# Patch embedding of a small vision model: f32 products replaced by three products of rounded high and low parts

## The chip, the cores and the metric

The kernel runs on one core of one Trainium2 chip. The metric is the device time of one execution in microseconds. Three executions of the kernel before took 379.61, 381.12 and 382.11 us, so the median is 381.12 us. One execution was also recorded by the hardware profiler; it took 379.39 us.

## The reference

The program is a vision tower: patch embedding, layer norm, two small causal attentions, a mixture of 32 experts (8 chosen per token) with a shared one, a full attention, and a quantised feed-forward block, with residuals. Only the first step matters here:

```
x = data.reshape(b, C, HP, P, WP, P)                      # 16 images, 3 x 96 x 96, P = 16
x = x.transpose(0, 2, 4, 1, 3, 5).reshape(b, N, F)        # N = 36 patches of F = 768 numbers
x = jnp.einsum('bnf,df->bnd', x, W_lin) + b_lin           # W_lin is 256 x 768
cls = jnp.broadcast_to(class_token, (b, 1, D))
out = jnp.concatenate([cls, x], axis=1) + position_embeddings
```

So 576 patches, with a column left free for each of the 16 class tokens, make T = 592 token columns. The product has an inner length of 768 and 256 results per token. All of it is float32.

## The kernel before, in words

Features lie on the 128 partitions and tokens along the free axis. The 592 tokens are worked in two halves of 296 columns (`half(hf)`), and the 256 model features in two chunks of 128 (`c`). The inner length of 768 is cut into KT = 6 pieces of 128. One SBUF tensor, `region`, holds the six pieces of patches (`patches`, 128 x 592 each) and the six pieces of weights (`w_lin_sb`, 128 x 256 each). Later stages use the same memory for other things.

Each engine has its own program, and semaphores join them. At the start:

- SyncE issues the six patch transfers (L340), then weights of the two attentions and of the last feed-forward block (L341 to L346), and waits for the embedding before it issues more (L347, L348).
- ScalarE issues three weight pieces (L532), then the constants `cst`, `vec` and `nt` (L533 to L535), then the other three weight pieces (L537), then three small attention weights (L538 to L540). Only after these twelve issues does it reach its first computation. That is a one-element activation whose purpose is to load the activation table of the next function (`load_table`, L550); it stands behind waits for the constants.
- VectorE clears `zeros` (L874), waits for the constants, converts some of them to bf16 (`cstb`, L876, which also completes `s_init`), adds two tables into `posb` (L877), waits for the embedding's sums half by half (`s_tok`) and adds `posb` to them (`h`, L882).
- TensorE runs 16 products on zeros ahead of the data (`keep_busy`, START_BUSY = 16). Then it takes the pieces k = 0 to 5 in order. For each it waits until patches and weights have landed (`s_x[k]`) and issues four f32 products, half 0 then half 1, chunk 0 then chunk 1, into four accumulators in PSUM. The last piece tells VectorE when half 0 and half 1 are summed.
- GpSimd sets a few small buffers (L399 to L405) and waits for the embedding.

After that follows the first norm: TensorE sums the means of `h` half by half (`s_h`), VectorE subtracts (`xc`, L777), ScalarE squares (`sq`, L562), TensorE sums the squares, ScalarE and VectorE make the scale, and VectorE applies it (`xn`, L792). Every step waits for the one before, for half 0 first. Every matmul of the kernel is recorded at one helper line, L1090.

In the expert stage of the kernel, products are already made of parts: ScalarE copies a tile into float32r, a rounded 32-bit format (`wh`, `ah`, `xh`: the high part), another engine subtracts the rounded copy from the original (`wl`, `al`, `xl`: the low part), and TensorE adds high x high, high x low and low x high (`three`). `split_all` is the float32r buffer of that stage and is not used before it.

Of the kernel before, what the change touches and what calls it, by code (L numbers as in the profile page):

```python
# [9 lines left out]
T = B * S  # L10
D = 256
P = 128
C = D // P
KT = 3 * PATCH * PATCH // P
HEADS, KVH, HD = 16, 4, 16
LAT = 64
HALF = T // 2
# [24 lines left out]
LEAD = 3  # L42
ATTENTION_BUSY = 5

QK_UNITS = ((0, 0), (1, 0), (2, 0), (2, 1), (0, 1), (1, 1))
ACT_VARIANTS = 2
WPIECES, VPIECES = 8, 8
WPIECE, VPIECE = C * FF // WPIECES, B * D // VPIECES
VZ = 1 + VPIECES
# [28 lines left out]
def program(nc, x, w_lin, consts, consts_bf, vecs, g_wq, g_down, g_k, g_v, g_wo, l_wq, l_wk, l_wv, l_wo,  # L78
            gate_w, experts, qkv_w, out_w, w1, w2, weights, out):
    f32, f32r, bf16 = mybir.dt.float32, mybir.dt.float32r, mybir.dt.bfloat16  # L80
    ALU, ACT, AX = mybir.AluOpType, mybir.ActivationFunctionType, mybir.AxisListType

    with ExitStack() as ctx:
        def sb(name, shape, dt=f32):
            return ctx.enter_context(nc.sbuf_tensor(name, shape, dt))

        def sem(name):
            return ctx.enter_context(nc.semaphore(name))
# [4 lines left out]
        patches = region[:, 0:KT * T].rearrange("p (k t) -> p k t", k=KT)  # L93
        w_lin_sb = region[:, KT * T:KT * (T + D)].rearrange("p (k d) -> p k d", k=KT)
# [79 lines left out]
        split_all = sb("split_all", [P, 2 * NRING * EW], f32r)  # L174
# [3 lines left out]

        pairs_r = split_all[:, 0:P]

        wb_flat = wb[:].rearrange("p r t -> p (r t)")
        qvar = [[z.rearrange("p (g t) -> p g t", g=4) for z in zs] for zs in
                ([wb_flat[:, c * C * T:(c + 1) * C * T] for c in range(C)],
# [22 lines left out]
        ps = [psum[:, i, :] for i in range(8)]  # L206

        def const(name, rows=P):
            a, b = CONST_COLS[name]
            return cst[0:rows, a:b]  # L210
# [8 lines left out]
        def half(hf):  # L219
            return slice(hf * HALF, (hf + 1) * HALF)  # L220
# [3 lines left out]


        s_x = [sem(f"patches_loaded{k}") for k in range(KT)]
        s_cst = sem("constants_loaded")
        s_attn_w = [sem(f"attention_weights_loaded{a}") for a in range(2)]
        s_wo_w = sem("output_weights_loaded")
# [292 lines left out]
        def _(act_e):  # L522
# [5 lines left out]
                ins.then_inc(s_act_own, 1)  # L528
                act_e.wait_ge(s_act_own, own[0])

            for k in range(LEAD):
                act_e.dma_start(w_lin_sb[:, k, :], w_lin[:, k, :]).then_inc(s_x[k], 16)  # L532
            act_e.dma_start(cst[:], consts).then_inc(s_cst, 16)  # L533
            act_e.dma_start(vec[:], vecs).then_inc(s_cst, 16)
            act_e.dma_start(nt[:, 0:NBF], consts_bf).then_inc(s_cst, 16)  # L535
            for k in range(LEAD, KT):
                act_e.dma_start(w_lin_sb[:, k, :], w_lin[:, k, :]).then_inc(s_x[k], 16)  # L537
            act_e.dma_start(down_sb[:], g_down).then_inc(s_attn_w[0], 16)  # L538
            act_e.dma_start(gk_sb[:], g_k).then_inc(s_attn_w[0], 16)
            act_e.dma_start(gv_sb[:], g_v).then_inc(s_attn_w[0], 16)  # L540
            act_e.wait_ge(s_init, 8)
            act_e.wait_ge(s_cst, 48)

# [34 lines left out]
            def key_variants(a, hf):  # L578

                act_e.wait_ge(s_qk, a * NPROJ + QK_UNITS.index((2, hf)) + 1)  # L580
                if a == 1:
                    act_e.wait_ge(s_s, PAIRS)
                for g in range(ACT_VARIANTS):
                    ins = nc.scalar.activation(km[:, 0, g, half(hf)], sq[:, 0, half(hf)], ACT.Copy,  # L584
# [128 lines left out]
            for hf in range(2):  # L713
                for m in range(C):
                    ins = nc.scalar.activation(h[:, m, half(hf)], ps[2 * m + hf][:, 0:HALF], ACT.Copy)
# [13 lines left out]
            for b in range(4):  # L729
# [3 lines left out]
                for j in range(2):  # L733
                    rows = slice(64 * j, 64 * j + S)
                    ins = nc.scalar.activation(v16[rows, 4 * b:4 * b + 4, :, j, :],
                                               ps[VALUE_BANKS[b]][rows, :].rearrange("p (i h d) -> p i h d", i=4, h=HEADS // 2),
                                               ACT.Copy)
# [24 lines left out]
        def _(dve):  # L762
# [8 lines left out]
            def bc(ap, dims):  # L771
                return ap.broadcast_to(dims)
# [39 lines left out]
            def qk_units(a):  # L812
# [6 lines left out]
                for u in range(NPROJ + 1):  # L819
# [22 lines left out]
                    if u >= 2 and QK_UNITS[u - 2][0] == 2:  # L842

                        hf = QK_UNITS[u - 2][1]
                        for g in range(ACT_VARIANTS, 4):
                            ins = nc.vector.tensor_scalar(km[:, 0, g, half(hf)], sq[:, 0, half(hf)],
# [25 lines left out]


            nc.vector.memset(zeros[:], 0.0).then_inc(s_zero, 1)  # L874
            dve.wait_ge(s_cst, 48)
            nc.vector.tensor_copy(cstb[:], nt[:, 0:NBF]).then_inc(s_init, 1)  # L876
            link(nc.vector.tensor_tensor(posb[:].rearrange("p c s -> p (c s)"), vector("pos"), vector("base"),  # L877
                                         ALU.add))
            for hf in range(2):
                dve.wait_ge(s_tok, hf + 1)  # L880
                for c in range(C):
                    ins = nc.vector.tensor_tensor(  # L882
                        h[:, c, half(hf)].rearrange("p (b s) -> p b s", s=S),
                        ps[2 * c + hf][:, 0:HALF].rearrange("p (b s) -> p b s", s=S),
                        bc(posb[:, c, :].unsqueeze(1), [P, HB, S]), ALU.add)
# [6 lines left out]
            for a in range(2):  # L892
# [8 lines left out]
                for hf in range(2):  # L901
# [3 lines left out]
                    for m in range(C):  # L905
                        ins = nc.vector.tensor_tensor((x0, tmp)[a][:, m, half(hf)], x0[:, m, half(hf)],
                                                      ps[4 + 2 * m + hf][:, 0:HALF], ALU.add)
# [29 lines left out]
            for t in range(TT):  # L937
                for g in range(GROUPS):
                    ins = nc.vector.max(top[:, t, g, :], choice[:, t, g * PER_GROUP:(g + 1) * PER_GROUP])
# [19 lines left out]
            for t in range(TT):  # L959
                ins = nc.vector.max(top[:, t, 0, :], masked[:, t, :])  # L960
            link(ins)
            for t in range(TT):
                ins = nc.vector.match_replace(repl[:, t, :], top[:, t, 0, :], masked[:, t, :], -3.0e38)
# [44 lines left out]
            for hf in range(2):  # L1008
# [5 lines left out]
                for c in range(C):  # L1014
                    for g in range(4):
                        ins = nc.vector.tensor_scalar(kvar[:, c, g, half(hf)], kt[:, c, half(hf)],
                                                      const("onehot4")[:, g:g + 1], None, ALU.mult)
# [16 lines left out]
            for hf in range(2):  # L1034
                dve.wait_ge(s_wo, 4 + hf + 1)
                for m in range(C):
                    ins = nc.vector.scalar_tensor_tensor(h[:, m, half(hf)], ps[4 + 2 * m + hf][:, 0:HALF],
                                                         outb[:, m:m + 1], h[:, m, half(hf)],
                                                         ALU.add, ALU.add)
# [16 lines left out]
            for ch in range(FC):  # L1056
                dve.wait_ge(s_hid, ch + 1)
                ins = nc.vector.tensor_reduce(peak[:, ch:ch + 1], hid[:, ch, :], AX.X, ALU.max,
                                              apply_absolute_value=True)
# [6 lines left out]
            for ch in DVE_CHUNKS:  # L1066
                ins = nc.vector.tensor_scalar(hid[:, ch, :], hid[:, ch, :], inv[:, 3:4], ROUND, ALU.mult, ALU.add)
# [8 lines left out]
            for m in range(C):  # L1076
                ins = nc.vector.tensor_scalar(x0[:, m, :], h[:, m, :], b2s[:, m:m + 1], None, ALU.add)
            link(ins)
            for hf in range(2):
                dve.wait_ge(s_f2, hf + 1)  # L1080
                for m in range(C):
                    ins = nc.vector.scalar_tensor_tensor(x0[:, m, half(hf)], ps[2 * m + hf][:, 0:HALF], sxw[:, 1:2],
                                                         x0[:, m, half(hf)], ALU.mult, ALU.add)
# [4 lines left out]
        def _(pe):  # L1088
            def mm(out_, lhsT, rhs, start, stop):
                return nc.tensor.matmul(out_, lhsT, rhs, start=start, stop=stop, skip_group_check=True)  # L1090
# [273 lines left out]
            pe.wait_ge(s_zero, 1)  # L1364
            keep_busy(7, START_BUSY, zeros[:, 0:P], zeros[:, 0:HALF])
            for k in range(KT):
                pe.wait_ge(s_x[k], 32)
                for hf in range(2):
                    for c in range(C):
                        ins = mm(ps[2 * c + hf][:, 0:HALF], w_lin_sb[:, k, c * P:(c + 1) * P],  # L1370
                                 patches[:, k, half(hf)], k == 0, k == KT - 1)
                    if k == KT - 1:
                        ins.then_inc(s_tok, 1)


            pe.wait_ge(s_init, 8)
# [29 lines left out]
            for t in range(TT):  # L1406
                if t == HALF // P:
                    pe.wait_ge(s_xn, 6)
                for c in range(C):
                    ins = mm(ps[6][:, t * EXPERTS:(t + 1) * EXPERTS], xn[:, c, t * P:(t + 1) * P],  # L1410
                             gate_sb[:, c, :], c == 0, c == C - 1)
# [75 lines left out]
            for u in range((UNITS - 1) // NRING * NRING, UNITS):  # L1487
                i = u % NRING
# [10 lines left out]
            for hf in range(2):  # L1499
                pe.wait_ge(s_xn, 6 + hf + 1)  # L1500
                for part in range(2):
                    for c in range(C):
                        bank = ps[4 * (1 - part) + 2 * c + hf][:, 0:HALF]
                        for k in range(C):
                            ins = mm(bank, qkv_sb[:, k, part * D + c * P:part * D + (c + 1) * P],
                                     xn[:, k, half(hf)], k == 0, k == C - 1)
# [12 lines left out]
            for ch in range(FC):  # L1519
                if ch >= 2:  # L1520
                    pe.wait_ge(s_hid, ch - 1)
                for hf in range(2):
                    for c in range(C):
                        ins = mm(ps[4 + 2 * (ch % 2) + hf][:, 0:HALF], w1q[:, c, ch * P:(ch + 1) * P],
                                 xq[:, c, half(hf)], c == 0, c == C - 1)
# [6 lines left out]
            for n, ch in enumerate(order):  # L1532
# [4 lines left out]
                for hf in range(2):  # L1537
                    for m in range(C):
                        ins = mm(ps[2 * m + hf][:, 0:HALF], w2q[:, ch, m * P:(m + 1) * P],
                                 hidq[:, ch, half(hf)], n == 0, n == FC - 1)  # L1540
# [128 lines left out]
```

## Time and profile before

| what | value |
|---|---|
| median of three executions | 381.12 us |
| profiled execution, its own time | 379.39 us |
| span of the profiled execution, first to last instruction | 377.6 us |
| mean granted TensorE clock | 0.995 |
| TensorE matmul busy | 349.9 us, 93% |
| TensorE weight load busy | 292.7 us, 78% |
| VectorE busy | 231.7 us, 61% |
| ScalarE busy | 179.4 us, 48% |
| GpSimd busy | 137.5 us, 36% |

The span is 1.8 us shorter than the time of the same execution; the rest lies before its first and after its last instruction. Matmul records overlap, since a matmul lasts longer than the distance to the next one, so the distance between starts is the rate. An f32 product of the program appears as two MATMUL records, a float32r or bf16 product as one. Busy shares are averages over stages with different limits; the change concerns the first 18 us of 377.6.

### The profile page before, as it was taken

Reading aid. Unit: us, or ns where it says so; the run is one execution under the profiler, and the core shown is the slowest. Engines: PE = TensorE matmul, PEld = TensorE weight load, DVE = VectorE, ACT = ScalarE, POOL = GpSimd, SP = SyncE. Lnnn points to the kernel's source line nnn. Section 1 sums busy time; section 2 is a strip of 40 time slices with the busy share of each in tenths; the row PEclk is TensorE's granted clock in tenths of the full one; section 3 lists DMA queues with packets and bytes.
Section 4 is the critical chain, followed back from the end, with each engine's and each line's share of the span. In section 5 each row is a group of like instructions: output and inputs, shape, how many; then the busy total and the mean of one; then the engine's idle time right before and its main releaser. Section 6 shows DMA issues by size and latency. Waiting matters only on the chain.

```text
span 377.6 us, 9798 instructions
## 1 busy us (share of the span) xinstructions
PE 349.9 (93%) x3916; PEld 292.7 (78%) x3916; DVE 231.7 (61%) x495; ACT 179.4 (48%) x353; POOL 137.5 (36%) x144
## 2 busy tenths in 40 slices
PE   8999898899898899999999999999999999889664
PEld 6655665568667899999999999999997788656333
DVE  0265689786879355555555555555554663666686
ACT  0156944487473244444444444444445774224270
POOL 0035852270260266665656544443310013410021
PEclk9999999999999999999999999999999999999899
DMA  8940001000550224444454544545200000000001
GB/s 295 366 144 0 3 6 30 0 3 3 169 169 2 90 97 142 141 146 148 148 147 148 143 139 127 146 133 152 80 1 2 0 2 3 5 3 0 0 2 66
DMA packets 14865, 32.08 MB, mean 85 GB/s; under 512 B 2480, under 2 KB 4464, under 8 KB 14576
## 3 DMA queue, kind: packets, MB, share of 16 engines
q1 hardware_dynamic: 12592, 29.66, 24.8%
q10 hardware_dynamic: 2240, 1.95, 1.5%
q8 instruction: 24, 0.39, 0.4%
q14 instruction: 9, 0.07, 0.1%
HBM read 30.91 MB, written 0.69 MB: 84 GB/s over the span
## 4 chain that ended last, share of the span: by engine, by line
PE 72%; DVE 14%; ACT 5%; DMA 3%; issue 3%; ACTq 1%; DVEq 0%
PE psum L1090 72%; DMA region<-in_w_lin 2%; DVE xn L792 1%; DVE rc L857 1%; DVE nt L786 1%; ACT region L749 1%; DVE nt L788 1%; DVE nt L789 1%; DMA wb<-weights 1%; DVE km L1072 1%; ACT km L584 1%; DVE pk L797 1%; DVE xc L777 1%; ACT sq L562 1%; ACT ars L565 1%
## 5 line engine op out<-in xcount | busy, mean ns | idle before, releaser
L1090 PE MATMUL psum<-xh,split_all 128*128 128x296 f32 x544 | 122.6, 299 | 1.8 <-DVE rt L986 1.8
L464 POOL TENSOR_TENSOR split_all<-km,split_all 128x768 fp32r<-128x768 f32 x34 | 63.7, 1876 | 85.0 <-ACT split_all L670 85.0
L1090 PEld LDWEIGHTS psum<-xh,split_all 128*128 128x128 f32 x544 | 91.7, 188 | 2.3 <-DVE rt L986 2.1
L1090 PE MATMUL psum<-xl,split_all 128*128 128x296 f32 (+1 forms) x288 | 85.1, 300 | 0.2 <-ACT e L641 0.2
L690 ACT ACTIVATE ah<-rt 128x296 fp32r<-128x296 f32 x68 | 30.7, 451 | 78.4 <-DVE rt L986 71.9
L1090 PEld LDWEIGHTS psum<-xl,split_all 128*128 128x128 f32 (+1 forms) x288 | 53.1, 187 | 1.1 <-POOL xl L507 0.4
L988 DVE TENSOR_TENSOR al<-rt,ah 128x296 fp32r<-128x296 f32 x64 | 30.0, 468 | 33.1 <-ACT ah L690 33.1
L1090 PE MATMUL psum<-ah,split_all 128*128 128x296 f32 x272 | 48.4, 300 | 1.3 <-ACT ah L690 1.3
L983 DVE TENSOR_TENSOR rb<-psum,wb 128x296 f32<-128x296 f32 x64 | 29.9, 467 | 31.8 <-ACT psum L688 28.1
L1090 PEld LDWEIGHTS psum<-ah,split_all 128*128 128x128 f32 x272 | 40.6, 188 | 1.8 <-ACT ah L690 1.8
L986 DVE TENSOR_TENSOR rt<-rb,psum 128x296 f32<-128x296 f32 x64 | 29.6, 463 | 5.2
L688 ACT ACTIVATE psum<-psum 128x296 f32<-128x296 f32 x64 | 25.7, 401 | 12.9 <-PE psum L1090 12.7
L670 ACT ACTIVATE split_all<-km 128x768 fp32r<-128x768 f32 x34 | 28.3, 833 | 4.2 <-DMA km<-in_experts 4.1
L1090 PE MATMUL psum<-al,split_all 128*128 128x296 f32 x136 | 29.9, 301 | 0.1
L641 ACT ACTIVATE e<-psum 101x592 f32<-101x592 f32 x24 | 15.7, 663 | 24.4 <-PE psum L1090 24.3
L507 POOL TENSOR_TENSOR xl<-mx,cst 128x592 fp32r<-128x592 f32 x8 | 9.6, 1199 | 46.0 <-DVE mx L1027 46.0
L1090 PE MATMUL psum<-cstb 128*128 128x296 bf16 (+1 forms) x196 | 25.8, 303 | 0.0
L1090 PEld LDWEIGHTS psum<-al,split_all 128*128 128x128 f32 x136 | 22.2, 189 | 0.6 <-POOL al L470 0.6
L1090 PE MATMUL psum<-region 128*128 128x296 f32 x80 | 21.5, 420 | 0.8 <-DMA region<-in_w_lin 0.4
L857 DVE RECIPROCAL rc<-psum 128x148 f32<-128x148 f32 x16 | 17.3, 1082 | 8.0 <-PE psum L1090 6.4
L1090 PEld LDWEIGHTS psum<-cstb 128*128 128x128 bf16 (+1 forms) x196 | 14.9, 101 | 8.9 <-issue 4.0
L1090 PE MATMUL psum<-sq,cst 128*128 128x296 f32 x64 | 19.6, 425 | 1.0 <-ACT sq L562 0.8
(176 smaller groups left out, 530.7 us busy)
## 6 DMA issues: line engine op xcount, KB each, us to landing
km<-in_experts SPq DMA_DIRECT2D x34, 384.0 KB, 4.0
wb<-weights SPq DMA_DIRECT2D x32, 296.0 KB, 3.7
w_sb<-in_w SPq DMA_DIRECT2D x2, 1024.0 KB, 11.6
region<-in_x SPq DMA_DIRECT2D x6, 296.0 KB, 5.3
region<-in_w_lin ACTq DMA_DIRECT2D x6, 128.0 KB, 6.3
qkv_sb<-in_qkv_w SPq DMA_DIRECT2D x1, 768.0 KB, 4.7
cst<-in_consts ACTq DMA_DIRECT2D x1, 502.5 KB, 6.4
out<-x SPq DMA_DIRECT2D x2, 148.0 KB, 2.1
```

The costliest lines, as they stand in the source:

```text
L464: nc.gpsimd.tensor_tensor(wl[i], ring[i], wh[i].bitcast(f32), ALU.subtract)\
L507: nc.gpsimd.tensor_tensor(dg[:, p % 2, :, :], mx[:, p % 2, :].unsqueeze(2).broadcast_to([P, HEADS, S]), const("minus_ident").unsqueeze(1). ...
L562: nc.scalar.activation(sq[:, :, half(hf)], src[:, :, half(hf)], ACT.Square).then_inc(s_sq, 1)
L641: nc.scalar.activation(e[0:ROWS, p % 2, 0:EC].rearrange("p (k n) -> p k n", k=2), psum[0:ROWS, sb0:sb0 + 2, 0:HALFPOS * S], ACT.Exp, scale ...
L670: nc.scalar.activation(wh[i], ring[i], ACT.Copy).then_inc(s_wsh, 1)
L688: nc.scalar.activation(gate, ps[bank][:, 0:HALF], ACT.Silu).then_inc(s_sg, 1)
L690: nc.scalar.activation(ah[:, j, :], act[:, j, :], ACT.Copy).then_inc(s_ah, 1)
L857: link(nc.vector.reciprocal(rc[:], bank[:, G4 * S:2 * G4 * S]))
L983: nc.vector.tensor_tensor(gu[:, j, :], gate, weight, ALU.mult).then_inc(s_mulc, 1)
L986: nc.vector.tensor_tensor(act[:, j, :], gu[:, j, :], ps[5][:, 0:HALF], ALU.mult).then_inc(s_act, 1)
L988: nc.vector.tensor_tensor(al[:, j, :], act[:, j, :], ah[:, j, :].bitcast(f32), ALU.subtract)\
L1090: return nc.tensor.matmul(out_, lhsT, rhs, start=start, stop=stop, skip_group_check=True)
```

## The change

The six pieces are now converted before they are multiplied. ScalarE rounds the weight piece (128 x 256) and each half of the patch piece (128 x 296) to float32r; VectorE subtracts to get the low parts, in the same order. TensorE makes three products for each one it made before: high x high, low weight x high patches, high weight x low patches. The parts live in three slots in `split_all`; ScalarE may fill a slot again once TensorE has told it (`s_pmm`) that the products of that slot are done. The six weight transfers are issued together, ahead of the constants.

```diff
+PATCH_SLOTS = 3
...
+        PW = 2 * (T + D)
+        pslot = [split_all[:, i * PW:(i + 1) * PW] for i in range(PATCH_SLOTS)]
+        px_hi, px_lo = [s_[:, 0:T] for s_ in pslot], [s_[:, T:2 * T] for s_ in pslot]
+        pw_hi, pw_lo = [s_[:, 2 * T:2 * T + D] for s_ in pslot], [s_[:, 2 * T + D:PW] for s_ in pslot]
...
-            for k in range(LEAD):
+            for k in range(KT):
                 act_e.dma_start(w_lin_sb[:, k, :], w_lin[:, k, :]).then_inc(s_x[k], 16)
             act_e.dma_start(cst[:], consts).then_inc(s_cst, 16)
             act_e.dma_start(vec[:], vecs).then_inc(s_cst, 16)
             act_e.dma_start(nt[:, 0:NBF], consts_bf).then_inc(s_cst, 16)
-            for k in range(LEAD, KT):
-                act_e.dma_start(w_lin_sb[:, k, :], w_lin[:, k, :]).then_inc(s_x[k], 16)
             act_e.dma_start(down_sb[:], g_down).then_inc(s_attn_w[0], 16)
             act_e.dma_start(gk_sb[:], g_k).then_inc(s_attn_w[0], 16)
             act_e.dma_start(gv_sb[:], g_v).then_inc(s_attn_w[0], 16)
+            for k in range(KT):
+
+                i = k % PATCH_SLOTS
+                act_e.wait_ge(s_x[k], 32)
+                if k >= PATCH_SLOTS:
+                    act_e.wait_ge(s_pmm, k - PATCH_SLOTS + 1)
+                nc.scalar.activation(pw_hi[i], w_lin_sb[:, k, :], ACT.Copy).then_inc(s_pwh, 1)
+                for hf in range(2):
+                    nc.scalar.activation(px_hi[i][:, half(hf)], patches[:, k, half(hf)], ACT.Copy).then_inc(s_pxh, 1)
             act_e.wait_ge(s_init, 8)
             act_e.wait_ge(s_cst, 48)
...
             nc.vector.memset(zeros[:], 0.0).then_inc(s_zero, 1)
+            for k in range(KT):
+
+                i = k % PATCH_SLOTS
+                dve.wait_ge(s_pwh, k + 1)
+                nc.vector.tensor_tensor(pw_lo[i], w_lin_sb[:, k, :], pw_hi[i].bitcast(f32), ALU.subtract).then_inc(s_pwl, 1)
+                for hf in range(2):
+                    dve.wait_ge(s_pxh, 2 * k + hf + 1)
+                    nc.vector.tensor_tensor(px_lo[i][:, half(hf)], patches[:, k, half(hf)],
+                                            px_hi[i][:, half(hf)].bitcast(f32), ALU.subtract).then_inc(s_pxl, 1)
             dve.wait_ge(s_cst, 48)
...
             for k in range(KT):
-                pe.wait_ge(s_x[k], 32)
+                i = k % PATCH_SLOTS
+                pe.wait_ge(s_pwh, k + 1)
+                for hf in range(2):
+                    pe.wait_ge(s_pxh, 2 * k + hf + 1)
+                    for c in range(C):
+                        mm(ps[2 * c + hf][:, 0:HALF], pw_hi[i][:, c * P:(c + 1) * P], px_hi[i][:, half(hf)], k == 0, False)
+                pe.wait_ge(s_pwl, k + 1)
                 for hf in range(2):
                     for c in range(C):
-                        ins = mm(ps[2 * c + hf][:, 0:HALF], w_lin_sb[:, k, c * P:(c + 1) * P],
-                                 patches[:, k, half(hf)], k == 0, k == KT - 1)
+                        mm(ps[2 * c + hf][:, 0:HALF], pw_lo[i][:, c * P:(c + 1) * P], px_hi[i][:, half(hf)], False, False)
+                    pe.wait_ge(s_pxl, 2 * k + hf + 1)
+                    for c in range(C):
+                        ins = mm(ps[2 * c + hf][:, 0:HALF], pw_hi[i][:, c * P:(c + 1) * P], px_lo[i][:, half(hf)],
+                                 False, k == KT - 1)
                     if k == KT - 1:
                         ins.then_inc(s_tok, 1)
+                if k < KT - PATCH_SLOTS:
+                    ins.then_inc(s_pmm, 1)
```

## Rows read from the trace of the kernel before

**Rows 1.** Page, chain of waits by engine; then its pieces in time (start, length).
```profile
PE 72%; DVE 14%; ACT 5%; DMA 3%; issue 3%; ACTq 1%; DVEq 0%
...
3.71 7.90 DMA region<-in_w_lin
...
11.65 6.25 PE psum L1090 x24
```

**Rows 2.** Timeline, embedding and what follows: start us, length us, engine, line, operation.
```profile
5.01 6.24 PE L1090 MATMUL psum<-region 128*128 128x296 f32 x24
...
11.65 6.25 PE L1090 MATMUL psum<-region 128*128 128x296 f32 x24 [0.41 <-DMA region<-in_w_lin]
...
17.02 1.76 DVE L882 TENSOR_TENSOR h<-psum,posb 128x296 f32<-128x296 f32 x4 [5.92 <-PE psum L1090]
...
18.00 2.23 PE L1090 MATMUL psum<-h,cst 128*128 128x296 f32 x8
```

**Rows 3.** Timeline of ScalarE's queue, transfer issues, first and last among twelve.
```profile
0.74 1.38 ACTq L532 DMA_DIRECT2D region<-in_w_lin  x3
...
2.15 0.45 ACTq L533 DMA_DIRECT2D cst<-in_consts  x1
...
3.71 1.56 ACTq L537 DMA_DIRECT2D region<-in_w_lin  x3
...
6.47 0.61 ACTq L540 DMA_DIRECT2D gv_sb<-in_g_v  x1
```

**Rows 4.** Timeline of ScalarE, its first table load; then all loads grouped.
```profile
10.76 1.28 ACT L550 ACT_TABLE_LOAD   x1 [10.76 <-DMA nt<-in_consts_bf]
...
12.05 0.20 ACT L550 ACTIVATE spare<-eps 128x1 f32<-128x1 f32 x1
...
L550 ACT ACT_TABLE_LOAD x11 | 14.1, 1283 | 10.9 <-DMA nt<-in_consts_bf 10.8
```

**Rows 5.** Groups by line and shape, ScalarE (busy us, mean ns); then two timeline rows.
```profile
L690 ACT ACTIVATE ah<-rt 128x296 fp32r<-128x296 f32 x68 | 30.7, 451 | 78.4 <-DVE rt L986 71.9 <-DVE rt L932 6.5
L670 ACT ACTIVATE split_all<-km 128x768 fp32r<-128x768 f32 x34 | 28.3, 833 | 4.2 <-DMA km<-in_experts 4.1
...
40.88 0.45 ACT L611 ACTIVATE rs<-rs 128x296 f32<-128x296 f32 x1
41.23 0.96 ACT L584 ACTIVATE km<-sq,cst 128x296 f32<-128x296 f32 x2
```

**Rows 6.** Groups by line and shape, VectorE, the subtractions of the expert stage.
```profile
L988 DVE TENSOR_TENSOR al<-rt,ah 128x296 fp32r<-128x296 f32 x64 | 30.0, 468 | 33.1 <-ACT ah L690 33.1
L923 DVE TENSOR_TENSOR xl<-xn,xh 128x592 fp32r<-128x592 f32 x2 | 1.5, 770 | 0.1
```

**Rows 7.** Busy by stretch: length; PE, PEld, DVE, ACT, POOL; PEclk, DMA, GB/s.
```profile
5.02:17.90 12.88, 12.47 (x49) 8.93 (x48) 1.23 (x4) 1.49 (x2) 0.00 (x0) 1.00 1.05 406
180.00:200.00 20.00, 20.00 (x149) 20.00 (x149) 11.41 (x25) 9.53 (x21) 12.34 (x14) 1.00 0.47 143
```

**Rows 8.** Timeline: TensorE starting on a high part that ScalarE has just made.
```profile
120.61 0.45 ACT L690 ACTIVATE ah<-rt 128x296 fp32r<-128x296 f32 x1 [2.61 <-DVE rt L932]
...
121.11 0.57 PEld L1090 LDWEIGHTS psum<-ah,split_all 128*128 128x128 f32 x4 [1.18 <-ACT ah L690]
```

**Rows 9.** Timeline of TensorE: bf16 products of one shape, after pauses and without.
```profile
1.09 4.13 PE L1090 MATMUL psum<-zeros 128*128 128x296 bf16 x16 [1.09 <-DVE zeros L874]
...
22.93 1.95 PE L1090 MATMUL psum<-cstb 128*128 128x296 bf16 x14
...
352.07 0.38 PE L1090 MATMUL psum<-cst,pk 128*1 128x128 f32 x2 [3.35 <-DVE pk L1046]
...
353.14 2.48 PE L1090 MATMUL psum<-cstb 128*128 128x296 bf16 x10
...
368.12 1.91 PE L1090 MATMUL psum<-km,w2q 128*128 128x296 bf16 x12 [1.44 <-DVE km L1072]
```

**Rows 10.** Busy by stretch, columns as in Rows 7, around the pauses of TensorE.
```profile
353.20:353.40 0.20, 0.20 (x3) 0.14 (x3) 0.16 (x1) 0.00 (x0) 0.00 (x0) 0.88 0.00 0
...
356.70:356.90 0.20, 0.20 (x3) 0.16 (x2) 0.00 (x0) 0.20 (x1) 0.00 (x0) 0.84 0.00 0
...
366.60:368.20 1.60, 0.17 (x2) 0.08 (x2) 1.57 (x3) 1.60 (x3) 1.51 (x3) 1.00 0.00 0
```

More of the change, by code:

```diff
@@ L226, in program @@
         s_x = [sem(f"patches_loaded{k}") for k in range(KT)]
+        s_pwh = sem("patch_weights_high_parts_ready")
+        s_pxh = sem("patch_high_parts_ready")
+        s_pwl = sem("patch_weights_low_parts_ready")
+        s_pxl = sem("patch_low_parts_ready")
+        s_pmm = sem("patch_products_summed")
         s_cst = sem("constants_loaded")
```

## The prediction

> **What bounds the kernel now.** I read the chain of waits first. TensorE holds 72% of it, and in the opening it runs through the weight transfer of piece 3 and the 24 matmul records behind it [rows 1]. The timeline of the first 20 us shows what that means: TensorE multiplies from 5.01 us, pauses 0.41 us for piece 3, and is done at 17.90 us; VectorE adds `posb` to half 0 from 17.02 us, and the means follow at 18.00 us [rows 2]. From there every step of the norm waits for the one before, so the number to follow is the start of that first add: **17.02 us**. Whatever moves it moves the end of the kernel by as much, because the later stages do not look back at the opening. Nothing else in the kernel is edited.
>
> Next, the rates. In the embedding 49 records take 12.47 us busy, and two records are one f32 product, so a product costs 0.52 us. In the expert stage, where products are float32r of the same 128x296 shape, 149 take 20.00 us: 0.134 us each [rows 7]. Three of them cost 0.40 us. The 24 products become 72 and 12.5 us become 9.65 us; that is the change's gain, 2.85 us if nothing else moved, plus the 0.41 us pause.
>
> **When TensorE can start.** It used to start on landed data at 5.01 us. Now it needs a high part from ScalarE, and ScalarE first issues its twelve transfers. The edit reorders them but keeps all twelve, and the last is issued from 6.47 to 7.08 us [rows 3]. ScalarE is free at 7.08 us.
>
> Its first activation then meets an engine with no activation table. The trace has 11 table loads of 1.283 us, and the first stands directly ahead of the first activation of the program, 1.29 us before it [rows 4]. No copy in the trace is preceded by one, but none comes first either. Bounds: 0 and 1.29 us. I take 1.29, because the row nearest in kind is the program's first activation. The load at L550 is for another function and stays, so there are twelve. First copy: 8.4 us.
>
> The Trainium skill, page "ScalarE: Activation LUTs", section "What ACT_TABLE_LOAD costs", puts a switch at 1.283 us plus a drain of 1.38 us, 2.66 us in all; by that the start would be 1.4 us later than in my sum. The trace agrees with the load and not with the drain here: the next activation starts 1.29 us after the load does [rows 4].
>
> Copy of the weight piece, 256 columns: between 451 ns at 296 and 833 ns at 768 the slope is 0.81 ns per column, so 0.42 us. A following activation starts about 0.35 us after a 296-column one of 0.45 us, so some 0.1 us before its end [rows 5]. The first patch half thus runs from about 8.7 to 9.15 us. TensorE reacts 0.05 us after a high part is done [rows 8]: **first product at 9.2 us**, 4.2 us later than now.
>
> **Who sets the pace afterwards.** Per piece ScalarE needs 0.32 + 0.35 + 0.35 = 1.0 us (1.3 if nothing overlaps) [rows 5]. VectorE subtracts 256, 296 and 296 columns; 468 ns at 296 and 770 ns at 592 give 1.02 ns per column [rows 6], so 0.43 + 0.47 + 0.47 = 1.37 us. TensorE needs 12 x 0.134 = 1.61 us. TensorE is the slowest, so it waits only inside the first piece, where the low parts come about 0.1 us late. The slot wait does not bite either: ScalarE wants slot 0 back at 8.4 + 3 x 1.0 = 11.4 us, and piece 0 is multiplied by 9.2 + 1.7 = 10.9. With slower products it comes a little later, and ScalarE still has two pieces in hand.
>
> **The sum.** The sum of half 0 is complete after product 68 of 72: 9.2 + 0.1 + 67 x 0.134 + 0.30 (length of the last) = 18.6 us. Now the add starts about 0.1 us behind such an end, so 18.7 against 17.02: **+1.7 us**. The order inside the last piece favours half 0 less than before, and that is in the 68.
>
> **The clock.** From 1.09 us TensorE runs 16 products on zeros, at 0.25 us apart; 14 products of the same shape take 1.95 us at 22.93 us [rows 9]. So the opening runs at the lower level, 1.2 GHz, though the column of granted clock has no record of it there, and the higher one is there about when the data arrive. After the change there is no work between 5.2 and 9.2 us, a pause of 4.0 us. The trace has one pause like it: 3.35 us before 352.07 us, then little work, and at 353.3 us the granted clock falls to half and returns at about 356.8 us [rows 10]; ten products take 2.48 us there [rows 9]. A pause of 1.44 us left the clock at 1.00 [rows 9, 10]. 4.0 us is nearer to the first, so I take one such stretch of 3.4 us at 1.2 GHz. Each us of it does 4 products in place of 7.4 and costs 1 - 0.134/0.25 = 0.46 us: **+1.5 us**. Bounds: 0, and all 68 products at 0.25 us, 68 x 0.116 = 7.9 us.
>
> Together +3.2 us. Against the profiled execution's own time, 379.39, that is 382.6 us; its median of runs is 1.7 us above it, so against 381.12 I forecast **384.3 us**.
>
> **The parts at nothing.** The earlier weight transfers: the pause of 0.41 us for piece 3 was real, but now piece 3 is wanted by ScalarE at 11.4 us and by TensorE after 14 us, so they buy nothing; ScalarE's start is set by the count of issues, not their order. SyncE's queue is not touched. The constants land later by 384 KB at about 406 GB/s [rows 7], 1 us; VectorE now wants them after its 18 subtractions, not before 8.85 + 8.2 = 17.0 us, and had them at 10.7. Cast and `posb` (0.5 us together) then run while TensorE does its last products; that cover is 1.6 us, more with a low clock, and without it they would cost up to 0.5 us. ScalarE's table load for the norm now comes behind its copies and the cast, at about 17.3, and ends at 18.8; the squares are wanted at about 21.8. GpSimd and SyncE wait for the embedding and have slack of tens of us at their next deadlines.
>
> **Rivals.**
> - *The clock stays up.* A pause of 4.0 us has only one near precedent. Then +1.7: 382.8 us.
> - *The low clock lasts longer: slower.* The place is the run of products from 9.2 us. At the program's start the low level lasted 4.1 us from the first product [rows 9], longer than 3.4. From 4.6 us on ((3.8 - 1.7)/0.46) the loss passes 1% of the time; two stretches of 3.4 us cost 3.1 + 1.7 = 4.8: 385.9 us. For it: products start and stop in the first piece while the low parts arrive. Against: at 1.2 GHz TensorE needs 3 us a piece and never waits.
> - *The table load holds ScalarE twice as long*, by a drain behind it. +3.2 + 1.4: 385.7 us. The page above says so; rows 4 speak against it.
> - *No table load ahead of a copy, clock stays up.* The pause is 2.7 us: +0.4, 381.5 us.
> - *The change does what its arithmetic promises.* This needs ScalarE to convert before its issues end. With copies from the landing of piece 0, 5.0 + 0.9 + 0.1 + 9.3 + 0.1 = 15.4: -1.6, 379.5 us. Rows 3 are against it: issues stand ahead in the same program.
>
> **How the numbers follow.** Chances: forecast 0.41, clock up 0.25, longer low clock 0.23, double load 0.02, no load 0.06, full gain 0.03. A measurement of this kernel tells a change from none at about 1%, 3.8 us. Slower by more than that holds the longer low clock, the double load and the upper part of the forecast (low for 4.6 us in place of 3.4): 0.33. Faster by more than 1% is out of reach of every case, even the full gain; 0.03 for what I do not see. Within 1%: 0.64. The range runs from 381.0 (clock up or no load, less 0.5 us for ends I placed too late) to 387.0 (two low stretches and a us of spread between executions, whose three runs span 2.5 us); outside it lie the full gain and a longer low clock still.
>
> **What would show it.** In the trace after: ScalarE's last issue near 7.1 us and a table load behind it; twelve loads; first high product near 9.2 us; starts 0.134 us apart once the clock is up, 0.25 before; no idle time of TensorE for low parts after piece 0; the first `posb` add between 18.7 and 20.5 us; everything behind it as before, only shifted. I am wrong if the first copy starts before 7 us, if VectorE's subtractions take over 1.6 us a piece, or if the clock is down past piece 1.

## The result and the profile after

The change made the kernel slower. Twenty executions took 385.6 us in the median (383.11 to 388.51), twenty of the kernel before 380.53 us. The ratio is 1.0128, 95% interval 1.0102 to 1.0153, or 3.9 to 5.8 us. The forecast was 384.3 us, inside 381.0 to 387.0, with 0.33 on a loss of over 1%, and the loss was over 1%. The forecast of the change was less close than that of the time: +3.2 us, where +4.9 us was measured by the ratio (the medians are 5.1 us apart). Some 0.6 us of the miss is hidden by luck, since the forecast started from 381.12 us, the median of three executions, and twenty gave 380.53. Medians in this document are over all executions; ratios and their intervals leave out the few that took over 1.5% more than the fastest of their kernel. The profiled execution took 386.48 us, its span 384.7 us.

The timeline of the opening of the kernel after (start us, length us, engine, line, operation). The rows answer to [rows 2, 3, 4]:

```profile
0.75 3.21 ACTq L543 DMA_DIRECT2D region<-in_w_lin  x6
...
1.09 4.12 PE L1117 MATMUL psum<-zeros 128*128 128x296 bf16 x16 [1.09 <-DVE zeros L892]
...
6.72 0.61 ACTq L549 DMA_DIRECT2D gv_sb<-in_g_v  x1
7.36 1.28 ACT L556 ACT_TABLE_LOAD   x1 [7.36 <-issue]
8.65 0.42 ACT L556 ACTIVATE split_all<-region 128x256 fp32r<-128x256 f32 x1
8.98 0.78 ACT L558 ACTIVATE split_all<-region 128x296 fp32r<-128x296 f32 x2
9.10 0.43 DVE L897 TENSOR_TENSOR split_all<-region,split_all 128x256 fp32r<-128x256 f32 x1 [8.07 <-ACT split_all L556]
...
9.55 11.43 PE L1117 MATMUL psum<-split_all 128*128 128x296 f32 x72 [4.34 <-ACT split_all L558]
...
12.92 0.42 ACT L556 ACTIVATE split_all<-region 128x256 fp32r<-128x256 f32 x1 [1.20 <-PE psum L1117]
...
17.77 0.24 DVE L903 CAST cstb<-nt 128x165 bf16<-128x165 f32 x1
...
20.56 1.58 DVE L909 TENSOR_TENSOR h<-psum,posb 128x296 f32<-128x296 f32 x4 [2.41 <-PE psum L1117]
```

Read from the top: twelve issues, then a table load, then the first copy; TensorE idles 4.34 us between its zeros and its first product, and once it has begun, its 72 products have no idle time. The first `posb` add starts at 20.56 us, 3.54 us later than the 17.02 of [rows 2].

The chain of waits of the kernel after, its pieces in order of time, tells who is to blame for the start. In [rows 1] a transfer stood here:

```profile
0.75 0.41 ACTq L543
...
6.72 0.61 ACTq L549
7.33 0.03 issue
7.36 1.28 ACT L556
8.64 0.01 issue
8.65 0.42 ACT split_all L556
9.07 0.35 ACT split_all L558
9.42 0.14 issue
9.55 10.90 PE psum L1117 x68
```

The chain now starts with ScalarE issuing transfers, where before it ran through the landing of weights. Next the busy time by stretch, columns as in [rows 7], with the granted clock as the eighth figure:

```profile
9.00:9.40 0.40, 0.00 (x0) 0.00 (x0) 0.30 (x1) 0.40 (x3) 0.00 (x0) 0.80 1.02 399
9.40:12.40 3.00, 2.85 (x11) 2.88 (x12) 3.00 (x9) 2.33 (x8) 0.00 (x0) 0.50 1.04 392
12.40:12.80 0.40, 0.40 (x3) 0.40 (x3) 0.07 (x1) 0.00 (x0) 0.00 (x0) 0.68 1.33 436
12.70:20.90 8.20, 8.20 (x61) 8.05 (x60) 4.20 (x12) 4.79 (x11) 0.00 (x0) 1.00 0.68 269
...
121.90:125.10 3.20, 3.20 (x14) 3.04 (x14) 2.88 (x27) 2.02 (x4) 0.00 (x0) 0.50 0.00 0
139.00:142.20 3.20, 3.20 (x14) 3.20 (x14) 1.76 (x4) 1.70 (x4) 2.17 (x2) 0.50 0.11 42
```

The clock falls during the pause, at 9.24 us by the 0.80 of the first row, and is at 1.2 GHz for 3.4 us. Products run in the last 3.1 us of it: 11 of them between 9.4 and 12.4 us, against 61 in 8.2 us at 2.4 GHz. The last two rows lie far behind the change. They are part of the 3.6 us by which this span grew beyond the opening (384.7 - 377.6 - 3.54); the experiments below ask whether they belong to the change.

### The profile page after: what moved, and what is told of

Same layout as the page of the kernel before. It is cut to its first block, busy times and chain, and to the rows that moved or that the text cites. A ratio compares the mean times of both kernels' runs of the same rounds, so it can differ in the third digit from the quotient of the medians.

```text
span 384.7 us, 9892 instructions
## 1 busy us (share of the span) xinstructions
PE 352.5 (92%) x3940; PEld 298.1 (77%) x3940; DVE 240.1 (62%) x513; ACT 187.1 (49%) x372; POOL 137.5 (36%) x144
## 4 chain that ended last, share of the span: by engine, by line
PE 71%; DVE 15%; ACT 6%; issue 3%; ACTq 2%; DMA 1%; POOL 0%; DVEq 0%
PE psum L1117 71%; DVE xn L810 1%; DVE h L939 1%; DVE nt L804 1%; ACT region L767 1%; DVE nt L807 1%; DVE nt L806 1%; DMA wb<-weights 1%; DVE rc L875 1%; DVE rc L886 1%; ACTq L543 1%; DVE pk L815 1%; DVE km L1099 1%; ACT L568 1%; ACT km L602 1%
## 5 line engine op out<-in xcount | busy, mean ns | idle before, releaser
L1117 PE MATMUL psum<-xh,split_all 128*128 128x296 f32 x544 | 124.3, 303 | 1.9 <-DVE rt L1013 1.9
L1117 PEld LDWEIGHTS psum<-xh,split_all 128*128 128x128 f32 x544 | 93.1, 191 | 2.2 <-DVE rt L1013 2.1
L1117 PE MATMUL psum<-xl,split_all 128*128 128x296 f32 (+1 forms) x288 | 86.1, 303 | 0.8 <-POOL xl L518 0.8
L1117 PEld LDWEIGHTS psum<-xl,split_all 128*128 128x128 f32 (+1 forms) x288 | 53.9, 189 | 1.7 <-POOL xl L518 1.1
L1117 PEld LDWEIGHTS psum<-sq,cst 128*128 128x128 f32 x64 | 11.3, 189 | 6.4 <-ACT sq L580 2.9
```

## The experiments

All were timed beside runs of the kernel before on the same chip: 380.98 us in the median of 35 runs for the first four, 380.88 us in 29 runs for the second four.

**a1_bridge: no pause.**

```diff
-START_BUSY = 16
+START_BUSY = 46
```

> After, with 46 products on zeros ahead of the patches in place of 16, so that TensorE works through the pause. Theory 'late start and low clock': high products still start near 9.5 us, but 0.134 us apart from the first; the first posb add starts near 19.0 us in place of 20.56 (1.5 us of clock gone), +2.0 us against before's 17.02, and the time is 1.5 us under after. Rival 'the conversions set the pace, not the clock': product spacing stays near what it was, with idle time of TensorE for low parts in every piece, and the time stays at after's, 385.6 us.

Timeline of its TensorE and VectorE, then the stretch of its products:

```profile
1.08 8.54 PE L1117 MATMUL psum<-zeros 128*128 128x296 bf16 x46 [1.08 <-DVE zeros L892]
...
9.36 10.06 PE L1117 MATMUL psum<-split_all 128*128 128x296 f32 x72
...
18.99 1.59 DVE L909 TENSOR_TENSOR h<-psum,posb 128x296 f32<-128x296 f32 x4 [2.41 <-PE psum L1117]
```
```profile
9.36:19.40 10.04, 10.04 (x75) 9.82 (x72) 6.97 (x21) 6.80 (x18) 0.00 (x0) 1.00 0.92 352
```

The same 72 products take 10.06 us in place of 11.43, and the add comes at 18.99 us. Of the 1.57 us gained there, 0.2 us is the first product being earlier (9.36 against 9.55); 1.37 us is the clock. The kernel took 382.62 us, ratio 1.0034 (1.0002 to 1.0067), 3.0 us under after's 385.6, which was timed in another series. That is twice the 1.5 us expected from one profile; c1 below shows that the opening of after can lose more than that. So the pause costs the clock, and the conversions don't set the pace: no product of the 72 waited.

**a2_const_on_sync: ScalarE free after six issues.**

```diff
 @block.sync
             for k in range(KT):
                 sp.dma_start(patches[:, k, :], x[:, k, :]).then_inc(s_x[k], 16)
+            sp.dma_start(cst[:], consts).then_inc(s_cst, 16)
+            ... vec, nt, down_sb, gk_sb, gv_sb in the same way
 @block.scalar
-            act_e.dma_start(cst[:], consts).then_inc(s_cst, 16)
-            ... and the five others
```

> After, with the six transfers that are not patches or patch weights (constants, latent weights) issued by SyncE behind its six patch transfers instead of by ScalarE. Theory 'late start': ScalarE issues six, is free at 4.0 us, loads its table until 5.3, and TensorE starts at 6.1-6.3 us, 3.3 us earlier; its pause shrinks to 1 us, after which the clock stays up as after the 1.44 us pause of the trace of before. Posb add at 15.7 us, 1.3 us before that of before; time 4.5 to 5 us under after, 0.5 to 1.5 under before. Rival 'transfers bound the opening': the pieces land later than TensorE wants them and the add does not come before 17 us; time near before.

Timeline:

```profile
3.95 1.28 ACT L556 ACT_TABLE_LOAD   x1 [3.95 <-issue]
...
6.14 10.05 PE L1117 MATMUL psum<-split_all 128*128 128x296 f32 x72 [0.93 <-ACT split_all L558]
...
15.76 1.59 DVE L909 TENSOR_TENSOR h<-psum,posb 128x296 f32<-128x296 f32 x4 [2.41 <-PE psum L1117]
```

Everything moved with the six issues: start 3.4 us earlier, pause 0.93 us, clock up throughout, add at 15.76 us. The median is 380.03 us, ratio 0.9984 (0.9948 to 1.0019). The loss of 1.3% is gone by moving six issues to another engine, with the same products; the gain over the kernel before, expected at 0.5 to 1.5 us, is not clear of none. Transfers do not bound it.

**a3_const_on_sync_bridge** is a2 with `START_BUSY = 23`.

> The same with 23 products on zeros in place of 16, which fills the pause of 1 us. If the clock is up in a2_const_on_sync already, no change against it (within 0.3 us in the opening); if the low clock lasts there, 1 to 1.5 us faster.

The add came at 16.36 us, 0.6 us later than in a2, because the zeros ran until after 6.5 us, past the first high part. So the expected 0.3 us was missed: the pause of 0.93 us needed no bridge. Its median is 379.52 us, ratio 0.9963 (0.9938 to 0.9989).

**a4_all_on_sync: ScalarE issues nothing.** SyncE issues patch piece and weight piece in turn, then the rest. ScalarE starts with

```diff
-            for k in range(KT):
-                act_e.dma_start(w_lin_sb[:, k, :], w_lin[:, k, :]).then_inc(s_x[k], 16)
+            act_e.wait_ge(s_zero, 1)
+            nc.scalar.activation(spare[:, 15:16], zeros[:, 0:1], ACT.Copy)
```

and there are 20 products on zeros.

> All transfers of the opening on SyncE (patch piece and weight piece in turn, then the rest); ScalarE issues none, loads its table at once by a one-element copy of zeros, and converts as pieces land; 20 products on zeros. Theory 'late start': TensorE starts at 5.5 to 6 us, 4 us earlier than in after; posb add at 15 to 15.5 us if pieces land in time (issues 0.47 us apart put the last piece at 6.3 us plus its flight), time about 1.5 to 2 us under before. Rival 'transfers bound': idle time of TensorE or ScalarE that ends in transfers, add at 16 us or later.

Timeline:

```profile
0.75 1.28 ACT L550 ACT_TABLE_LOAD   x1 [0.75 <-PEq L1699]
...
4.00 0.42 ACT L557 ACTIVATE split_all<-region 128x256 fp32r<-128x256 f32 x1 [1.76 <-DMA region<-in_w_lin]
...
5.65 10.06 PE L1118 MATMUL psum<-split_all 128*128 128x296 f32 x72
...
6.08 0.42 ACT L557 ACTIVATE split_all<-region 128x256 fp32r<-128x256 f32 x1 [0.98 <-DMA region<-in_w_lin]
...
15.28 1.59 DVE L910 TENSOR_TENSOR h<-psum,posb 128x296 f32<-128x296 f32 x4 [2.35 <-PE psum L1118]
```

The table load is hidden, piece 0 is converted as it lands, and the add starts 1.74 us before that of [rows 2]. ScalarE waits for the transfers of the first two pieces, the second time for 0.98 us, and once more for the constants, behind its copies; TensorE, once it has begun, never waits. Its start at 5.65 us is set by the 20 products on zeros: the first high part of a patch piece is done near 4.8 us (0.45 us after 4.33, when its copy starts). Fewer zeros were not tried. The median is 379.73 us, 1.3 us under that of the kernel before by the ratio, where 1.5 to 2 was expected; ratio 0.9965 (0.9939 to 0.9990). a3 and a4 beat both kernels, by about 0.35% against the kernel before, with each interval just clear of none. The two cannot be told apart.

**c1_after_again: the changed kernel, unedited.**

> The changed kernel once more, unedited, beside runs of the kernel before on one chip. The opening of its profile gave +3.5 us (posb add at 20.56 against 17.02), the median of its runs +5.1. Theory 'opening plus chance': the clock falls to half for stretches of 3.4 us in the middle of runs of either kernel, and the 1.5 us beyond the opening are such stretches; then the difference here lies anywhere from 3 to 5 us and, among executions with a granted clock of 0.99 and more, near 3.6. Rival 'the change costs 1.5 us in a later stage too': the difference is 5 us again, at equal clock as well.

Timeline and busy time by stretch of its profiled execution:

```profile
9.37 12.66 PE L1117 MATMUL psum<-split_all 128*128 128x296 f32 x72 [4.20 <-ACT split_all L558]
...
21.61 1.58 DVE L909 TENSOR_TENSOR h<-psum,posb 128x296 f32<-128x296 f32 x4 [2.41 <-PE psum L1117]
```
```profile
8.30:8.70 0.40, 0.00 (x0) 0.00 (x0) 0.00 (x0) 0.39 (x2) 0.00 (x0) 0.66 1.08 410
8.70:15.10 6.40, 5.73 (x23) 5.76 (x24) 4.55 (x12) 3.94 (x12) 0.00 (x0) 0.50 1.07 406
15.10:15.50 0.40, 0.40 (x5) 0.40 (x4) 0.00 (x0) 0.00 (x0) 0.00 (x0) 0.81 0.98 367
```

The same program, and the low clock lasts about 6.8 us in place of 3.4: the add comes at 21.61 us, 4.59 us after that of before. The median is 385.08 us, ratio 1.0099 (1.0063 to 1.0135), 2.4 to 5.1 us. So one kernel shows both openings, +3.5 and +4.6 us. Their mean, +4.05 us, lies inside the intervals of both comparisons (3.9 to 5.8 us, and 2.4 to 5.1 us here), though the medians of the first are 5.1 us apart. Two executions were profiled; the openings of the others are not known.

What of the stretches in the middle? Before has them too: of its 64 runs beside these experiments only 25 have a mean clock of 0.99 or more, and the mean over all is 0.986. The 28 runs of after have 0.979. Each stretch of 3.4 us takes 0.5 x 3.4 / 380 = 0.0045 off the mean, so after has about 1.5 more of them, which is what its two openings have. The kernels without the long pause (a1 to a4, b1, c4, c5) have means of 0.984 to 0.989, near that of before.

Among runs with a clock of 0.99 or more the medians are 379.80 (25 runs) and 383.85 (4 runs), 4.0 us apart, where the theory had 3.6. This comparison is weaker than it looks: the profiled execution of before has a mean clock of 0.995 with one low stretch, at 353 us; at 0.0045 for each, a run of after at 0.991 to 0.996 has at most two in all, its opening's included. It therefore has fewer of them elsewhere or a shorter one in the opening, and its difference from before is not that of the opening alone.

**b1_before_order_only**: the kernel before with `LEAD = 6`.

> The kernel before with only the order of the transfers changed: all six weight pieces ahead of the constants. Theory: the pause of 0.41 us for piece 3 goes, products run on from 5.0 us without one, posb add at 16.6 us, time 0.4 us less, hardly to be told from none. Rival 'the constants come too late': VectorE's cast and posb are wanted by 16.6 us and land near 11.7, so no loss; a loss would show as the add starting after a transfer.

Timeline:

```profile
4.83 12.12 PE L1090 MATMUL psum<-region 128*128 128x296 f32 x48
13.51 0.25 DVE L876 CAST cstb<-nt 128x165 bf16<-128x165 f32 x1 [12.48 <-DMA nt<-in_consts_bf]
...
16.07 1.76 DVE L882 TENSOR_TENSOR h<-psum,posb 128x296 f32<-128x296 f32 x4 [2.17 <-PE psum L1090]
```

The pause of 0.41 us is gone and the add starts at 16.07 us, 0.95 us earlier than in [rows 2] and 0.5 us earlier than expected: 0.18 us is an earlier first product, the rest a little less time per product. The constants land 2.8 us later and still in time. The ratio is 0.9984 (0.9957 to 1.0010), no difference that these runs can tell. This half of the change did no harm.

This run also answers what the two late rows of the kernel after asked. Here is the stretch from 100 to 145 us in before, in b1 and in a4, and then a part of it in b1:

```profile
100.00:145.00 45.00, 40.65 (x256) 34.98 (x256) 30.48 (x99) 21.95 (x40) 19.27 (x15) 1.00 0.35 111
100.00:145.00 45.00, 40.93 (x241) 35.73 (x240) 30.07 (x97) 21.05 (x38) 17.51 (x14) 0.92 0.34 106
100.00:145.00 45.00, 39.72 (x249) 34.05 (x249) 30.89 (x96) 21.66 (x40) 18.58 (x15) 1.00 0.35 112
...
117.60:120.40 2.80, 2.80 (x10) 2.21 (x8) 2.56 (x23) 0.94 (x3) 0.00 (x0) 0.50 0.03 6
```

b1 has no conversions and has low stretches there; a4 has all the conversions and none. So these stretches don't belong to the change.

**c4_f32_products_late: a1 with f32 products.** TensorE waits for the high parts, and before half 1 of each piece for the low parts too, but multiplies the originals.

```diff
-                    for c in range(C):
-                        mm(ps[2 * c + hf][:, 0:HALF], pw_hi[i][:, c * P:(c + 1) * P], px_hi[i][:, half(hf)], k == 0, False)
-                ... the products with low parts
+                    if hf == 1:
+                        pe.wait_ge(s_pwl, k + 1)
+                        pe.wait_ge(s_pxl, 2 * k + 2)
+                    for c in range(C):
+                        ins = mm(ps[2 * c + hf][:, 0:HALF], w_lin_sb[:, k, c * P:(c + 1) * P],
+                                 patches[:, k, half(hf)], k == 0, k == KT - 1)
```

> a1_bridge (46 products on zeros, so no pause) with the 72 products of parts replaced by the 24 f32 products of the kernel before, on the same waits for the high parts; the conversions still run, their results are not used. It measures the exchange of products alone. Theory: products start at 9.4 us as in a1_bridge and take 12.5 us in place of 9.7; 20 of 24 and 68 of 72 come before half 0 is summed, so the posb add moves from 18.99 to about 20.9 us, 1.9 to 2.0 us later; time 2 us over a1_bridge. Rival 'three products of parts save nothing, since waits between them eat it': add within 0.5 us of 18.99.

Timeline:

```profile
9.74 12.20 PE L1117 MATMUL psum<-region 128*128 128x296 f32 x48 [0.53 <-ACT split_all L558]
...
21.06 1.76 DVE L909 TENSOR_TENSOR h<-psum,posb 128x296 f32<-128x296 f32 x4 [3.07 <-PE psum L1117]
```

From first product to add it takes 11.32 us, against 18.99 - 9.36 = 9.63 us in a1. The 48 records follow each other without idle time, so the waits for low parts cost nothing. The exchange of products alone is worth 1.7 us on the path, a little under the 1.9 to 2.0 expected; the rest of the 2.07 us by which the add moves is a first product 0.38 us later. The median is 385.24 us, ratio 1.0094 (1.0061 to 1.0127); by the ratios that is 2.3 us over a1, which ran on another chip.

**c5_two_products: a1 without low weights x high patches.** It leaves the low part of the weights out of the result; the two lines with `pw_lo` in TensorE's program are gone.

> a1_bridge without the product of low weights and high patches (48 products in place of 72; the low part of the weights is left out of the result). Theory 'TensorE sets the pace, VectorE is close behind': TensorE needs 8 x 0.134 = 1.07 us a piece and VectorE, by the trace of a1_bridge, 1.09, so the two tie; last subtraction near 15.4 us, cast and posb behind it, add at 15.9 to 16.1 us in place of 18.99, time 3 us under a1_bridge. Rival 'the conversions already bind with 72': add at 18 us or later.

Timeline of VectorE:

```profile
14.44 0.42 DVE L897 TENSOR_TENSOR split_all<-region,split_all 128x256 fp32r<-128x256 f32 x1
14.77 0.84 DVE L900 TENSOR_TENSOR split_all<-region,split_all 128x296 fp32r<-128x296 f32 x2
15.53 0.24 DVE L903 CAST cstb<-nt 128x165 bf16<-128x165 f32 x1
15.68 0.23 DVE L904 TENSOR_TENSOR posb<-vec 128x74 f32<-128x74 f32 x1
16.20 1.58 DVE L909 TENSOR_TENSOR h<-psum,posb 128x296 f32<-128x296 f32 x4 [0.28 <-PE psum L1117]
```

With a third of the products gone the add moves from 18.99 to 16.20 us, 2.8 us, and VectorE idles only 0.28 us before it: the two engines tie there. With 72 products TensorE is the slower, by the 2.41 us that VectorE waits in a1. The median is 380.37 us, ratio 0.9965 (0.9934 to 0.9996), by the ratios 2.6 us under a1, where 3 was expected.

## Why the prediction came out as it did

Point by point, in the order of its steps:

- **First product at 9.2 us**: 9.55 us, and 9.37 in c1. The issues ended at 7.33 us in place of 7.08, since the weight transfers took longer to issue. The rest is small waits between steps.
- **A table load ahead of the first copy**: there, 1.28 us, with the copy 1.29 us after its start. The drain of 1.38 us that the Trainium skill has in the page "ScalarE: Activation LUTs", section "What ACT_TABLE_LOAD costs", did not show here either, and not where copies stand straight ahead of a load (load at 17.33 us in the kernel after, next activation at 18.62); that rival falls, and so does the one without a load.
- **TensorE sets the pace**: right; no idle time within 72 products. The price of VectorE was too high, 1.37 us a piece against 1.09 us between one piece's first subtraction and the next in a1, because I added lengths where consecutive instructions overlap. The slot wait that I put at nothing is there, 1.20 us in after and 0.53 and 0.55 us in a1, but it falls on ScalarE, which is ahead by then, and TensorE lost no time to it.
- **The exchange of products**: 2.85 us was the reckoning over the whole stage and about 1.9 us on the path to the add; c4 shows 1.7. The distance in a1 is 0.137 us in place of 0.134.
- **The clock**: it fell, for 3.4 us in one execution and 6.8 us in the other, and cost 1.37 and 2.6 us. Forecast for one stretch +1.5 and for two +3.1; the openings were +3.5 and +4.6 us in all, where I had +3.2 and +4.8. The forecast and its slower rival are therefore not two outcomes but two executions of one kernel. That is the step that was off: I gave the low clock one length, though the medians mix them. The mean of the two, near +4, lies over the 3.8 us that make 1%, and so I put too much on "within 1%".
- **Parts at nothing**: right in effect, wrong in one size. I had the constants 1 us late; b1 shows 2.8 us. They were covered all the same, by 4 us in after.
- **No later stage moves**: supported. If it holds, the difference of the runs is the shift of the first add in the profile. In eight of the nine comparisons the interval holds the shift. The ninth is the first series of the kernel after: its interval lies just above +3.54 and holds +4.05, the mean of the two openings. a1 and c4 carry all the conversions and lose no more than their openings.

| kernel | shift of the first add, us | difference of the runs, us (interval) |
|---|---|---|
| after, first series | +3.54 | +4.9 (3.9 to 5.8) |
| after again (c1) | +4.59 | +3.8 (2.4 to 5.1) |
| a1_bridge | +1.97 | +1.3 (0.1 to 2.6) |
| c4_f32_products_late | +4.04 | +3.6 (2.3 to 4.8) |
| a2_const_on_sync | -1.26 | -0.6 (-2.0 to 0.7) |
| a3_const_on_sync_bridge | -0.66 | -1.4 (-2.4 to -0.4) |
| a4_all_on_sync | -1.74 | -1.3 (-2.3 to -0.4) |
| b1_before_order_only | -0.95 | -0.6 (-1.6 to 0.4) |
| c5_two_products | -0.82 | -1.3 (-2.5 to -0.2) |

Late start, cheaper products and clock add up. From a1: the first product is 9.36 - 5.01 = 4.35 us later; from product to add it takes 9.63 us where before it took 12.01, 2.38 us less (1.7 of it by the products, the rest by the pause for piece 3 and a little spacing); that leaves +1.97 us. After has a start 0.2 us later still and 1.37 us of low clock: +3.54.

## What to carry to other kernels

When work is put in front of an engine's first instruction, ask what that engine is doing until then: here twelve transfer issues of half a microsecond each were free while ScalarE had nothing else to do, and cost 3 to 4 us once it had. An exchange that saves 1.7 us of products is worth it only if its conversions find an idle engine and a loaded table; move issues to the engine that waits anyway, and load the table while the first data are in flight. A warm-up is worth what stands directly behind it: if its successor moves, lengthen it or close the gap.

## What the runs showed of the hardware

- In a pause of 4.2 to 4.3 us on TensorE the clock fell, to stay at 1.2 GHz for 3.4 us in one execution and 6.8 us in another of the same kernel; one of 0.93 us was followed by no fall. What decides between the two lengths was not tried.
- Stretches of 3.4 us at half clock also occur in the middle of the kernel (14 products in 3.2 us at 139 us), near the same two places of its work. The one at 139 us begins within 0.2 us of the end of a pause of 1.90 us. The same pause, 1.84 us before 132.77 us in the trace of before, left the clock at 1.00. Of the ten traces seven have a stretch at one or both places, b1 among them, and three (before, a3, a4) at neither. What decides was not tried.
- These stretches are a part of the spread of 378.2 to 385.5 us of the kernel before, not all: its 15 runs with a mean clock of 0.994 or more still lie between 378.74 and 381.80 us.
- The first activation of the kernel after is a copy, and a table load of 1.28 us stands ahead of it; none stands ahead of a later copy.
